# Relative attention: from a four-unit plan with widened queries to a four-bank flow with parity-masked dense queries in row groups

## The reference, cut to what matters

```
x = layernorm(src, ln1)                     # src is itself layernorm(residual)
q, k, v = x@wq, x@wk, x@wv                  # 16 heads of 16 columns
p = pe @ wp                                 # 223 positions, 16 heads
ac = einsum('bihd,bjhd->bhij', q, k)
bd_full = einsum('bihd,phd->bhip', q, p)
bd = bd_full[:, :, i, i - j + 111]          # row i is shifted by i
att = softmax((ac + bd) * 0.25)
src = src + (att @ v) @ wo
moe = top-4 of 32 experts on layernorm(src, ln2)
out = residual + src + moe
```

## Time and profile before

| | |
|---|---|
| median of 3 runs | 4380.85 us (4376.88 to 4382.57) |
| profiled execution, its own time | 4381.62 us |
| its span | 4379.8 us |
| mean granted TensorE clock | 0.970 |
| busy over the span | PE 92%, PEld 64%, DVE 62%, ACT 43%, POOL 6% |
| relative attention | about 2875 to 3507 us of the span |

### The profile page before, as it was taken

How to read it: one execution, slowest core, us unless ns; L and a number is a source line. 1 busy time by engine, 2 the same in 40 slices (tenths; PEclk the granted TensorE clock), 3 DMA queues, 4 the chain that set the end, 5 groups by cost and what they waited for, 6 DMA issues and landing times. The chain is left out here.

```text
span 4379.8 us, 88099 instructions
## 1 busy us (share of the span) xinstructions
PE 4019.6 (92%) x30632; PEld 2820.5 (64%) x30632; DVE 2701.1 (62%) x5798; ACT 1889.5 (43%) x5106; POOL 267.5 (6%) x389
## 2 busy tenths in 40 slices
PE   7999899999999699887688888889999889999999
PEld 6887455555555466775455565568888756666666
DVE  5777465656655466776465555557777655555555
ACT  4777455555555232443234343346666611111111
POOL 0000111111111000111000000000000000000000
PEclk9999899999999799999899999989999989999999
DMA  6000000000000000000332222234444320000000
GB/s 142 0 0 0 17 16 16 12 16 12 16 16 8 1 0 0 1 0 4 66 65 61 59 63 60 40 89 128 128 124 128 109 78 5 5 5 5 6 5 9
DMA packets 178390, 165.50 MB, mean 38 GB/s; under 512 B 98681, under 2 KB 159106, under 8 KB 178050
## 3 DMA queue, kind: packets, MB, share of 16 engines
q1 hardware_dynamic: 172176, 144.62, 12.9%
q10 hardware_dynamic: 6002, 17.89, 1.6%
HBM read 75.49 MB, written 55.05 MB: 30 GB/s over the span
## 5 line engine op out<-in xcount | busy, mean ns | idle before, releaser
L2285 DVE SCALAR_TENSOR_TENSOR g_residual<-m_out,m_gate,g_residual 112x256 f32 (+1 forms) x1280 | 549.5, 479 | 419.5 <-PE m_out L2134 414.9
L2134 PE MATMUL m_out<-e_down,m_hidden 128*112 128x256 f32 x2560 | 603.3, 379 | 0.0
L2134 PEld LDWEIGHTS m_out<-e_down,m_hidden 128*112 128x112 f32 x2560 | 452.5, 177 | 192.3 <-issue 112.5
L2123 PE MATMUL m_hidden_bank<-m_xT,e_up 128*128 128x448 f32 x1280 | 537.5, 545 | 2.6 <-issue 2.6
L2185 ACT ACTIVATE m_hidden<-m_hidden_bank 128x448 f32<-128x448 f32 x256 | 139.3, 544 | 646.1 <-PE m_hidden_bank L2123 646.1
L1699 DVE TENSOR_REDUCE x_top<-x_scores 112x4 f32<-112x1500 f32 x128 | 219.9, 1718 | 266.2 <-PE x_scores L1555 263.8
L2123 PEld LDWEIGHTS m_hidden_bank<-m_xT,e_up 128*128 128x128 f32 x1280 | 240.1, 191 | 149.2 <-issue 133.1
L1112 ACT ACTIVATE x_probs<-x_held,x_minus_top 112x488 f32<-112x488 f32 x256 | 177.5, 694 | 264.0 <-DVE x_minus_top L1168 264.0
L1813 PE MATMUL r_ring<-w_pT,r_q 128*112 128x224 f32 x1024 | 240.3, 369 | 17.8 <-ACT r_by_position L821 13.4
L1023 PE MATMUL x_ring<-w_xkv,x_kv 128*122 128x512 f32 x512 | 233.4, 599 | 15.7 <-ACT x_k L821 15.0
L1016 PE MATMUL x_ring<-x_kv,w_xkv 128*128 128x488 f32 x512 | 240.4, 593 | 0.0
(11 more groups left out here) (286 smaller groups left out, 7478.8 us busy)
## 6 DMA issues: line engine op xcount, KB each, us to landing
by_position<-r_by_position SPq DMA_DIRECT2D x128, 392.0 KB, 3.1
r_bias<-by_position SPq DMA_DIRECT2D x128, 196.0 KB, 3.3
x_ctx<-in_ctx SPq DMA_DIRECT2D x64, 375.0 KB
x_kq_swapped<-x_kq_raw ACTq DMA_DIRECT2D x64, 243.5 KB, 3.6
x_slots<-x_kq SPq DMA_DIRECT2D x512, 30.4 KB
e_up<-in_L_ffn_keys SPq DMA_DIRECT2D x16, 256.0 KB, 6.0
e_down<-in_L_ffn_values SPq DMA_DIRECT2D x8, 512.0 KB, 6.8
g_residual<-in_x SPq DMA_DIRECT2D x4, 896.0 KB, 11.0
```

Of the source, the lines that this page charges most:

```text
L2123: ins = nc.tensor.matmul(hidden_bank[e % 2][:, 0:Q * T], M["up"][:, f, e, :], xT[par][:, f, :], start=(f == 0), stop=(f == DC - 1))
L2134: ins = nc.tensor.matmul(out_bank[2 * (e % 2) + i // 2][0:T, (i % 2) * D:(i % 2 + 1) * D], hidden[e % 2][:, i * T:(i + 1) * T], M["down"][ ...
L2285: nc.vector.scalar_tensor_tensor(row, out_bank[2 * (e % 2) + i // 2][0:T, (i % 2) * D:(i % 2 + 1) * D], gate[par][0:T, i, e:e + 1], row, A ...
```

## The change

It moves the relative attention to `stream`. Heads are kept dense, two in each row group of 32 rows, so the query is copied twice under a mask of parity (even heads, odd heads). For column block f, row group j and parity p the head is 8f + 2j + p. Positions and scores are made by matmuls of 32 rows in four row groups that write the four banks of one scores tile. This tile serves in turn the positions of heads 0 to 7 (pos0), those of heads 8 to 15 (pos1), and the scores. ScalarE copies each half of the positions in one instruction of 1792 columns, SyncE writes and reads the scratch in halves, and VectorE adds the bias, takes the maximum and subtracts it for all 16 heads in one instruction each. One exponential follows. The sums come from the ones in the values. The end is that of `Streamed`. The two additions to X leave the stage and one addition per chunk of four batches joins the last experts.

```diff
-class RelativeAttention(CausalAttention):
+class RelativeAttention(Streamed):
...
-        self.plan = Plan(4, ["xT"],
-                         {0: ["q", "stats", "k"], 1: ["p0", "again", "p2", "p1", "project"],
-                          2: ["p3", "p5", "p4", "scale", "v", "p6", "xT"], 3: ["p7", "spread"]}, late=["project"])
+        self.plan = Flow(4, [("stats", 0), ("q", 1), ("scores", 2), ("k", 1), ("again", 0), ("f0", 3), ("f1", 3), ("pos0", 1),
+                             ("top", 2), ("f2", 3), ("f3", 3), ("scale", 0), ("heads", 3), ("v", 1), ("onT", 4), ("pos1", 1),
+                             ("less", 2), ("back", 3), ("exp", 2), ("project", 4), ("xT", 0)],
+                         bankless=("stats", "again", "scale", "scores", "top", "less", "exp", "pos0", "pos1"))
...
     def sync(self, sp):
         def shift(b, par):
+            for c in range(3):
+                if c < 2:
+                    sp.wait_ge(self.placed[c], b + 1)
+                    sp.dma_start(self.scratch[par][c], self.by_position[0:T, c, :, :]).then_inc(self.written[c], 16)
+                if c > 0:
+                    sp.wait_ge(self.written[c - 1], b * 16 + 16)
+                    s = self.scratch[par][c - 1]
+                    src = bass.AP(s.tensor, s.offset + T - 1, [(8 * RPW - 1, T), (RPW, 8), (1, T)])
+                    sp.dma_start(self.bias[par][0:T, c - 1, :, :].rearrange("t j (p k) -> t (j p) k", k=T),
+                                 src).then_inc(self.bias_loaded[par][c - 1], 16)
...
     def pool(...):
+        elif name in ("pos0", "pos1"):
+            c = int(name[3])
+            pool.wait_ge(self.positioned[c], b + 1)
+            at_least(pool, self.added, b - 1)
+            pool.sem_inc(self.placed[c], 1)
...
     def pe(...):
+        elif name == "scores":
+            self.ready(pe, "k", b)
+            pe.wait_ge(self.positioned[1], b + 1)
+            for f in range(DC):
+                for p in range(2):
+                    for j in range(HS):
+                        rows = slice(SLOT * j, SLOT * (j + 1))
+                        at = 512 * j + (2 * f + p) * T
+                        ins = nc.tensor.matmul(self.scores[0:T, at:at + T], self.q[par][rows, p, f, :], self.k[par][rows, f, :],
+                                               start=True, stop=True)
+            ins.then_inc(self.scored, 1)
+        elif name in ("pos0", "pos1"):
+            f = int(name[3])
+            if f == 0:
+                self.ready(pe, "q", b)
+                at_least(pe, self.added, b)
+            else:
+                pe.wait_ge(self.positioned[0], b + 1)
+            for p in range(2):
+                for j in range(HS):
+                    rows = slice(SLOT * j, SLOT * (j + 1))
+                    at = 512 * j + p * RPW
+                    ins = nc.tensor.matmul(self.scores[0:T, at:at + RPW], self.q[par][rows, p, f, :], W["pT"][rows, f, :],
+                                           start=True, stop=True)
+            ins.then_inc(self.filled[f], 1)
+        elif name in ("f0", "f1", "f2", "f3"):
+            bank = ring.claim(pe, c, body)
+            pe.wait_ge(self.exped, b + 1)
...  (four transposes of the probabilities)
+        elif name == "heads":
+            bank = ring.claim(pe, c, body)
+            self.ready_all(pe, ("v", "f0", "f1", "f2", "f3"), b, c)
...
     def act(...):
+        elif name in ("pos0", "pos1"):
+            f = int(name[3])
+            act.wait_ge(self.filled[f], b + 1)
+            at_least(act, self.written[f], b * 16)
+            nc.scalar.activation(self.by_position[0:T, f, :, :].rearrange("t (j p) r -> t j (p r)", p=2),
+                                 self.scores[0:T, :].rearrange("t (j c) -> t j c", c=512)[:, :, 0:2 * RPW],
+                                 ACT.Copy).then_inc(self.positioned[f], 1)
+        elif name == "exp":
+            act.wait_ge(self.lessened, b + 1)
+            self.reuse(act, "f3", b)
+            nc.scalar.activation(self.probs[0:T, :, :], self.biased[0:T, :, :], ACT.Exp, scale=self.scale).then_inc(self.exped, 1)
...
     def dve(...):
         elif name == "again":
-            chain.link(self.norm_scale(dve, self.norm, b, S[0:T, b, :], X[0:T, b, :]))
-            nc.vector.tensor_tensor(X[0:T, b, :], X[0:T, b, :], S[0:T, b, :], ALU.add)
+            chain.link_apart(self.norm_scale(dve, self.norm, b, S[0:T, b, :], X[0:T, b, :]))
...
         elif name == "q":
             bank = ring.take(dve, c, body)
-            ring.freed(self.widen(self.q[par][:], bank[:, 0:DC * T], self.const("mask8"), DC, 8, T), c)
+            for p in range(2):
+                ins = nc.vector.tensor_scalar(self.q[par][:, p, :, :].rearrange("p f t -> p (f t)"), bank[:, 0:DC * T],
+                                              self.const("parity")[:, p:p + 1], None, ALU.mult)
+            ring.freed(ins, c)
+        elif name == "scores":
+            dve.wait_ge(self.scored, b + 1)
+            for f in range(2):
+                dve.wait_ge(self.bias_loaded[par][f], loads(b, par))
+            at_least(dve, self.exped, b)
+            nc.vector.tensor_tensor(self.biased[...], self.scores[...], self.bias[par][...], ALU.add).then_inc(self.added, 1)
+        elif name == "top":
+            dve.wait_ge(self.added, b + 1)
+            nc.vector.tensor_reduce(self.tops[0:T, :], self.biased[0:T, :, :], AX_X, ALU.max).then_inc(self.topped, 1)
+        elif name == "less":
+            dve.wait_ge(self.topped, b + 1)
+            nc.vector.tensor_tensor(self.biased[0:T, :, :], self.biased[0:T, :, :], bc(self.tops[0:T, :], 2, T),
+                                    ALU.subtract).then_inc(self.lessened, 1)
...
         elif name == "project":
             bank = ring.take(dve, c, body)
-            nc.vector.tensor_tensor(S[0:T, b, :], bank[0:T, 0:D], S[0:T, b, :], ALU.add)
-            ring.freed(nc.vector.tensor_tensor(X[0:T, b, :], bank[0:T, 0:D], X[0:T, b, :], ALU.add), c)
+            ring.freed(nc.vector.tensor_tensor(S[0:T, b, :], bank[0:T, 0:D], S[0:T, b, :], ALU.add), c)
...
@@ experts, VectorE, step scale @@
+                    if layer == 1:
+                        chain.link(nc.vector.tensor_tensor(X[0:T, rows, :], X[0:T, rows, :], SRC[0:T, rows, :], ALU.add))
```

More of the change, by code:

```diff
@@ L1747, in allocate @@
     def allocate(self, sb, sem):
[L1748 to L1755, removed]
@@ L1756, in allocate @@
-        self.written = [sem(f"written{u}") for u in range(HG)]
-        self.bias_loaded = [[sem(f"bias_loaded{i}_{u}") for u in range(HG)] for i in range(2)]
+        self.allocate_end(sb, sem)
+        self.norm, self.norm2 = self.allocate_norm(sb, sem), self.allocate_norm(sb, sem, "2")
+        self.xn, self.xT = sb("xn", [P, D]), sb("xT", [P, DC, T])
+        self.q = [sb(f"q{i}", [P, 2, DC, T]) for i in range(2)]
+        self.k = [sb(f"k{i}", [P, DC, T]) for i in range(2)]
+        self.v = [sb(f"v{i}", [P, H, SLOT]) for i in range(2)]
@@ new lines, in allocate @@
+        self.by_position = sb("by_position", [P, 2, 8, RPW])
+        self.bias = [sb(f"bias{i}", [P, 2, 4, 2 * T]) for i in range(2)]
+        self.biased, self.probs = sb("biased", [P, H, T]), sb("probs", [P, H, T])
+        self.tops = sb("tops", [P, H])
+        self.probsT = sb("probsT", [P, 4, 4 * T])
+        self.scratch = [[self.nc.dram_tensor(f"by_position_{i}_{c}", [T, 8, RPW], F32).ap() for c in range(2)] for i in range(2)]
+        self.positioned = [sem(f"positioned{c}") for c in range(2)]
@@ L1806, in pe @@
             self.pe_rows(pe, c, body, self.xT, W["rv"], T)
[L1807 to L1817 removed]
+        elif name == "scores":
+            self.ready(pe, "k", b)
+            pe.wait_ge(self.positioned[1], b + 1)
+            for f in range(DC):
+                for p in range(2):
[20 more added lines that the diff above has]
+        elif name in ("f0", "f1", "f2", "f3"):
+            j = int(name[1])
+            bank = ring.claim(pe, c, body)
+            pe.wait_ge(self.exped, b + 1)
+            for i in range(4):
+                ins = nc.tensor.transpose(bank[0:T, i * T:(i + 1) * T], self.probs[0:T, 4 * j + i, :],
+                                          self.const("ident", T)[:, 0:T])
+            ring.filled(ins, c)
+        elif name == "heads":
+            bank = ring.claim(pe, c, body)
+            self.ready_all(pe, ("v", "f0", "f1", "f2", "f3"), b, c)
+            for g in range(HG):
+                for a in range(HS):
+                    h = HS * g + a
+                    j, i = (h % 8) // 2, 2 * (h // 8) + h % 2
+                    ins = nc.tensor.matmul(bank[SLOT * a:SLOT * (a + 1), g * T:(g + 1) * T], self.v[par][0:T, h, :],
+                                           self.probsT[0:T, j, i * T:(i + 1) * T], start=True, stop=True)
+            ring.filled(ins, c)
+        elif name == "back":
+            self.pe_back(pe, b, c, body)
+        elif name == "onT":
+            self.pe_onT(pe, b, c, body)
+        elif name == "project":
```

(1 more changed line is left out.)

86 lines of the change are left out of this document (36 added, 50 removed).

## The result

The changed kernel is slower: 4451.06 us median (4443.71 to 4464.59), against 4381.71 for the kernel before on the same chip. The ratio is 1.0162, with a 95% interval of 1.0145 to 1.0179: 1.6% or 69 us. The profiled execution took 4443.71 us, its span 4441.9, 62 us above the span before.

A forecast was written before the change was run, and what follows sets the result against it. A one-frame loop through the bias's write and read was to bound it: 19.15 us plus 1.2 for the clock, 20.35 per batch. With ends 28.3 and 19.5, the stage takes 679 us, 46 more: 4427, range 4325 to 4510.

The forecast's parts named there:

- The signs: In the stage: bias addition idle 4 us or more per batch, additions 20 us apart, TensorE busy near half, clock 0.7 to 0.9.
- What leaves TensorE: Relative attention: position matmuls and scores lose 7.7 us, dense projection one more; TensorE needs about 10 us per batch, not 18.2.
- The loop: From one bias addition to the next, through pos0, heads, v, pos1, copies, write and read: 19.15 us per batch before clock cost.
- The transfers: Write and then read of half 1 in the loop: 8.2 us, with ends 6.6 and 9.5.
- The clock: TensorE's clock falls in its idle gaps: 3.8 us per batch more at half clock, of which 1.2 was taken.
- The ends: Start and end of the stage: 28.3 us through the first addition, 19.5 us after the last.
- The small parts: Additions in the last experts, additions leaving the stage, and lighter loads: 0 taken, at most 4 us in all.
- That the transfers grow by less: Rival: doubling the bytes adds 1 us, write and read take 6.6, clock holds; 17.55 us per batch, 4340 us; chance 0.15.
- That the bias is in time: Rival: the addition does not wait for the bias, leaving a loop of 15.0 us per batch; 4259 us; chance 0.10.
- Half clock throughout: Rival: TensorE stays at half clock in the stage; 22.9 us per batch, 4508 us; chance 0.15.
- The row groups do run side by side: The rival was that they don't: matmul bursts add 2 x 2.4 us to the loop, 24 us; chance 0.02.
- The rule on PSUM: Skill page: tiling speeds TensorE but not emptying PSUM; so read, the two 1.67 us copies in the loop would set the time.

The follow-up runs named there:

- the last version: Changed kernel with the bias used one frame later, the frame's order rewritten, and the statistics called again moved ahead of the first position scores: 4164.5 us, ratio 0.9504.
- The moved pos1: Changed kernel with the second position scores moved ahead of scale, heads, v and onT, nothing else changed: 4324.7 us, ratio 0.9870.
- the later bias: Changed kernel with the bias used one frame later than it is made, with three buffers: 4309.3 us, ratio 0.9833.
- the early read: Changed kernel with half 0 read once its write has landed, before the write of half 1: 4438.4 us, again 4439.0 beside 4457.5 for the changed kernel.
- the second profile: Profile of the unaltered changed kernel when measured again beside the kernel that reads half 0 early: 4457.5 us, ratio 1.0176 to the kernel before.
- the first comparison: The first measurement of the changed kernel against the kernel before: 4451.06 us, ratio 1.0162.

## Why the prediction was right, and where it was off

The direction, the mechanism and the place were right; the time of 4427 was 24 us short of 4451, inside the range. The signs came as named but for one: the addition waited 4.45 us for the bias, additions were 21 us apart and the clock was 0.78 to 0.82, but TensorE was busy for 66% of the stretch from 2940 to 3540 us and not near half, as work at half clock lasts longer. Step by step:

- **What leaves TensorE.** Sized right. The position scores take 1.03 us at full clock (1.0 forecast), the scores 1.05, and TensorE was no longer the bound. In the last version, at a clock of 1.00, it is busy for 0.877 x 12.07 = 10.6 us per batch, where 10 was forecast.
- **The loop.** Its work was right almost to the tenth: wake to second copy, 8.75 us forecast; from the table's full-clock values 0.15 + 1.17 + 1.665 + 3.16 + 1.09 + 1.665 = 8.90. The moved pos1 and the later bias both show that this ring sets the period: shorten it, and the period follows.
- **The transfers** were 8.4 us with the hop and the wake, and measured 8.68. The doubling of the bytes was the right term: 2.1 plus 0.4 for the read of half 0 in the way, 2.5 forecast, 2.8 shown. The 0.4 alone was shown as 0.68 by the early read.
- **The clock** is the step that was mis-sized: 1.2 us per batch, a third of the 3.8 of a whole frame at half clock, where 1.5 to 2.0 were measured. The third came from the thought that TensorE recovers in two busy stretches. In fact pos0 stands behind the longest gap (3.6 us on average, 4.0 forecast) and was at half clock, in whole or in part, in 26 of the 27 frames (21 in the second profile), and what lies between the copies was in 11 (19). With 0.33 here, 0.28 in the transfers and 0.15 in the work, the sum of 20.35 becomes the table's 21.13. Over all 31 periods the mean is 20.97, as the first and last are shorter; 31 times 0.62 is 19 us of the 24. The rest is mostly that the profiled execution, which this account follows, was 7.3 us below the median, less the 3.2 us that other parts of the span gave back.
- **The ends.** The first addition ended after 26.8 us (28.3 forecast), and the tail took 20.6 (19.5). 26.8 + 31 x 20.97 + 20.6 = 697.5.
- **The small parts** cost nothing, as taken: the experts are 1.2 us shorter, if anything.

**The rivals.** That the transfers grow by less fell with the halved bytes (5.86 against 8.68 us). The estimate that the Trainium skill gives (DMA: Bandwidth & Descriptors, section Anatomy of one DMA, worked out for another queue) was 6.8 us for the pair; the write took 4.5 and the read 3.4 us at its least, 7.9 together. From half the bytes to all of them the page's slope gives 1.4 us more (an estimate), and 2.8 were measured, so it is too small for these two. That the bias is in time was wrong for this kernel; made true by one frame more it gave 4309, and without the wait 4310, not 4259, since the rest of the ring is 16.6 to 16.9 us and not 15.0: the waits stay, and with them a clock of 0.90. Half clock throughout was too dark: the stage had 0.82 and 0.78. The row groups do run side by side (1.03 us for sixteen instructions, not 16 x 0.215). The rule on PSUM from the Trainium skill (TensorEngine Tiling (Array Packing), Performance Considerations) describes a fixed part of the ring, 2 x 1.67 us; it was not what decided, as moving other things by 4 us left the copies alone.

Where the saving on TensorE went is plain: some 7.6 us of its work per batch (18.2 before, 10.6 in the last version) did not count once the ring was closed, and the ring of one frame is 2.4 us longer than the old period.

## What to carry to other kernels

When a change makes the busiest engine faster, look for the ring that remains, write its members down from one instruction to its next occurrence, and ask which of them are there only by their place in the order: here one entry moved was worth 3%, one frame more of distance 3%, a frame more with a new order over 6%. Batching small transfers into large ones lengthens the last one, which is the one that is waited for. Where TensorE waits some 3 to 5 us in each period, as here, price what it does next at half clock, size a fill by the gaps of all frames and not by one frame's, and don't conclude from two single profiles on effects of that size.

## What was not expected of the hardware

- A wait costs more than its length: 2.8 us less of transfer took 4 us off the period, as the clock's cost, 1.5 to 2.0 us per batch before, fell to 0.4. Five matmuls without use, 3.9 us of work per batch, put the kernel 24 and 30 us below its two measurements without them.
- The clock's cost differs between executions of one program: 1.5 and 2.0 us per batch, which is 14 us over the stage, and the two spans are 13.8 us apart (4441.9 and 4455.7). Among the four executions of the first comparison the longest span, 4462.6, has the lowest mean clock of the core, 0.934, and the shortest, 4441.9, the highest, 0.943.
- A read of 392 KB issued 0.35 us ahead of a write of 784 KB on the same queue made the write land in 5.4 us in place of 4.4.
- GpSimd's instruction of one column took 2.26 us in place of 0.55 when it began during VectorE's subtraction of two SBUF operands. Moved away from the subtraction, it took 0.55 again. The Trainium skill (SBUF — State Buffer, section SBUF: two separate sides) says that the two engines share a pair of ports as an exclusive lock for a whole instruction, when VectorE's has two SBUF inputs and GpSimd's reads SBUF. The trace agrees: it ended 0.41 us after the subtraction.
